# The scaled rows of each image computed on VectorE instead of GpSimd, and two table steps moved ahead of the attention rows

## The chip, the cores and the metric

The kernel runs on one core of a Trainium2 chip. The metric is the device time of one launch in microseconds (us), lower is better. Engine names are those of the profile: PE is TensorE (PEld its weight loads), DVE is VectorE, ACT is ScalarE, POOL is GpSimd, SP is the sync engine, which starts most DMAs.

## The reference, cut to what matters

32 images of 224 x 224 pixels are cut into 1024 patches each, embedded in 64 numbers, passed through one attention head, a layer normalisation, and a feed-forward layer in which each token goes to one of 8 experts. An expert takes the tokens in order, over all images, until its capacity is full.

```python
h = patches @ W.T + b + pos                       # 32 x 1024 x 64
q, k, v = h @ Wq.T + bq, h @ Wk.T + bk, h @ Wv.T + bv
prob = softmax(q @ k.T / 8)                       # per image, 1024 x 1024
h = layernorm(h + prob @ v @ Wo.T + bo)
logits = h @ gate_w + gate_b
idx = argmax(softmax(logits))                     # one of 8 experts
pos = running count of idx over all 32768 tokens
y = relu(h @ w1[idx] + b1[idx]) @ w2[idx] + b2[idx]
out = layernorm(h + nan_to_num(y * prb * (pos < C)))
```

## The kernel before

**Windows.** The program runs in windows b = -2 to 33, one per image. Each engine has its own hand-ordered program `step(b, ...)`, and the engines meet only through semaphores. Window b computes the score matrix of image b, the row maxima of image b+1, the projections of images b+1 and b+2, and the end of attention of image b-1: PE turns the weighted sums to token rows (`turn_sums`, L618), DVE divides them by the softmax sums (`attend`, L1053 to L1058), the residual is added (`residual`, L1387, POOL), ACT squares, DVE sums (`sum_squares`, L1080), ACT takes the root (`norm_root`, L822 and L824), DVE computes the gate (`gate_logits`, `gate_gaps`, `gate_choice`, L1089 to L1111). In window b+1 DVE computes the slots of these tokens (`slot_read`, `probability`, `slot_index`, L1191 to L1206) and POOL scatters the rows to DRAM by indirect DMA (`scatter`, L1411). I count a window from the first matmul of `turn_sums` to that of the next.

**Experts.** From window 6 on, one chunk of four units of 256 tokens of some expert is read back and computed beside each window (`HOST`). Its last steps, all on DVE, are spread over the next two windows: `weigh` (L1213), `finite`, `to_numbers`, `residual_sum`, `centre`, `sum_of_squares`, `scaled` (L1259). POOL writes the finished rows out (`spread_out`, L1424).

**The table.** Every second image (2, 4, ... 28, 30, and 31) DVE works out which units are full and names them for the DMAs. In an even window b from 4 on, `full_units` (L1138 to L1144) and `past_experts` (L1149, L1152) run for image b-2 behind the row maximum of j = 2, and `name_units` follows at j = 3. In the next, odd, window `take_units` (L1182 to L1184) runs behind `attend`. So even windows carry `full_units`, odd ones `take_units`.

**DVE's order in a window.** j counts the eight row maxima (`row_max`, L1031) of the next image; each waits for two matmuls (L563, L565), and the other steps stand between them in a fixed order. Before the first stand `qk_low` (L1023), `shift` (L1037), the slots of image b-2 and, at j = 0, `key_steps` (L1016). ACT waits for `key_steps` to copy the keys (L781), then copies the weighted sums (`u_copy`, L809), and PE's `turn_sums` waits for that copy. The gate stands at j = 6 and 7 (from j = 5 on in windows without a chunk).

**POOL's order in a window** (7 < b < 31): four scatters of image b-2, the residual of image b-1, four scatters, five output transfers, `norm_rows` of image b-1 (rows times reciprocal deviation, 128 x 512, L1398, and the token numbers, 128 x 8, L1399), three output transfers. For images 30 and 31 (`LATE` is 30) the residual and the rows are already on DVE: `last_residual` (L1067) and `last_rows` (L1073, L1074).

Of the kernel before, what the change touches and what calls it, by code (L numbers as in the profile page):

```python
# [12 lines left out]
ALU = mybir.AluOpType  # L13
# [74 lines left out]
def build(nc, x, posT, wqk, wide, deep, w, out):  # L88
    slots = nc.dram_tensor("slots", (SLOTS, ROW), F32, kind="Internal").ap()
    with ExitStack() as ctx:  # L90
# [244 lines left out]
        pool_step = sem("pool_step")  # L335
        sd_ready = sem("sd_ready")
        last_rows_ready = sem("last_rows_ready")
# [45 lines left out]
        PS = 1  # L383
# [379 lines left out]
        def _(act):  # L763
# [52 lines left out]
            def norm_root(n):  # L816
                act.wait_ge(vs_ready, n + 1)
                if n >= 1:
                    act.wait_ge(tail_g, GS * (n - 1) + 1)
                    act.wait_ge(pool_step, min(n, LATE))  # L820
                    after(act, last_rows_ready, n - LATE)
# [138 lines left out]
        def _(dve):  # L960
# [100 lines left out]
            def last_residual(n):  # L1061

                dve.wait_ge(t_ready, n + 1)
                dve.wait_ge(pool_step, PS * LATE)
                after(dve, last_rows_ready, n - LATE)
# [4 lines left out]
            def last_rows(n):  # L1070
                p = n % 2
                dve.wait_ge(scattered[p], of_parity(n - 2, p, 16 * NT))
                dve.tensor_tensor(rows[:, p, :, 0:D], uc[:, :, 0:D], per_token(rstd[:, :], D), ALU.mult)  # L1073
                dve.tensor_scalar(rows[:, p, :, D + 1], rows[:, p, :, D + 1], float(2 * S), None, ALU.add)\  # L1074
                    .then_inc(last_rows_ready, 1)
# [186 lines left out]
            def late_step(n, q, back, done):  # L1262
# [13 lines left out]
                last_rows(n)  # L1276
# [15 lines left out]
            def step(b, c, third, has):  # L1292
# [16 lines left out]
                for j in range(NT):  # L1309
                    if j == 0 and has(2):  # L1310
                        key_steps(b + 2)
                    if has(1):
                        row_max(b + 1, q, j)
                    if j == 1 and has(-1):
                        attend(b - 1, q)
                    if b - 3 in TABLES[:-1] and j == 1:
                        take_units(b - 3)
                    if b - 2 in TABLES[:-1]:
                        if j == 2:
                            full_units(b - 2)  # L1320
# [11 lines left out]
                    if has(-1):  # L1332
# [4 lines left out]
                        if j == 6:  # L1337
                            gate_gaps(b - 1)
                        if j == 7:
# [29 lines left out]
        def _(pool):  # L1369
# [12 lines left out]
            def residual(n, p):  # L1382
# [3 lines left out]
                wait_apart(pool, sq_ready, n)  # L1386
                pool.tensor_tensor(uc[:, :, :], tt[:, :, :], hh[:, p, :, 0:CG], ALU.add)\  # L1387
                    .then_inc(uc_ready, 1)

            def counted(n, i, ins):  # L1390
                ins.then_inc(pool_step, 1)
                wait_apart(pool, pool_step, PS * n + i)

            def norm_rows(n, p):
                pool.wait_ge(rstd_ready, n + 1)
                if n >= 2:
                    pool.wait_ge(scattered[p], of_parity(n - 2, p, 16 * NT))
                pool.tensor_tensor(rows[:, p, :, 0:D], uc[:, :, 0:D], per_token(rstd[:, :], D), ALU.mult)  # L1398
                counted(n, 1, pool.tensor_scalar(rows[:, p, :, D + 1], rows[:, p, :, D + 1], float(2 * S), None,  # L1399
                                                 ALU.add))  # L1400

            def scatter(n, p, tiles):
                if 0 in tiles:
                    wait_apart(pool, prob_ready, n + 1)
                    wait_apart(pool, tail_g, GS * n + GS)
                    if n >= LATE:
# [124 lines left out]
```

## Time and profile before

| | us |
|---|---|
| median of 3 runs (lowest, highest) | 1059.79 (1058.4, 1060.67) |
| the profiled execution | 1059.04 |
| its span in the trace | 1057.1 |
| busy PE, DVE, ACT, POOL | 947.4, 871.8, 712.3, 635.8 |

The span is the time between the first and the last instruction of the profiled execution; 1.9 us of that execution's time lie outside it, and it was 0.75 us faster than the median. TensorE's granted clock is full in all windows that are looked at below (the column PEclk reads 1.00). A row of the timeline gives start, duration, engine, source line and operation, the tile written and those read; in brackets behind it, where there is one, the idle time of the engine before it and what ended it. Start times can overlap the end of the instruction before by some 0.1 us, since an instruction begins while the last results of the one before are still written.

### The profile page before, as it was taken

How to read it: one execution, taken by the hardware profiler on the slowest of the kernel's cores; microseconds unless marked ns; L12 is line 12 of the kernel's file. 1: busy time of each engine (PE TensorE's matmuls, PEld its weight loads, DVE VectorE, ACT ScalarE, POOL GpSimd, SP SyncE). 2: the span in 40 equal slices, each digit the busy share in tenths (PEclk: the TensorE clock that was granted, in tenths of full speed). 3: DMA queues.
4: the chain of work that ended last, by engine and by line, in shares of the span. 5: the costliest groups of instructions: out<-in, count | busy, mean ns of one | idle time of the engine just before them, and what ended most of it. 6: DMA issues, size and time to landing. Idle time of an engine off the chain costs nothing.

```text
span 1057.1 us, 19754 instructions
## 1 busy us (share of the span) xinstructions
PE 947.4 (90%) x6046; PEld 530.7 (50%) x6046; DVE 871.8 (82%) x1711; ACT 712.3 (67%) x1254; POOL 635.8 (60%) x624
## 2 busy tenths in 40 slices
PE   3799999999999999999999999999999999856740
PEld 2355545555555555555555555555555555433420
DVE  3667788789999999999999999999999999675561
ACT  2366655777777777777777777777777776636650
POOL 0004443346666666667776766666666777776775
PEclk9699999999999999999999999999999999958875
DMA  3332224333334333343334333433334332236200
GB/s 95 80 73 58 59 59 107 91 100 101 98 86 120 89 107 99 89 106 103 103 99 107 102 99 86 120 88 107 98 91 106 102 99 72 71 92 177 71 20 10
DMA packets 72504, 96.25 MB, mean 91 GB/s; under 512 B 15923, under 2 KB 52230, under 8 KB 72398
## 3 DMA queue, kind: packets, MB, share of 16 engines
q1 hardware_dynamic: 55566, 77.87, 29.0%
q0 software_dynamic: 16832, 17.11, 5.0%
q8 instruction: 49, 0.80, 0.3%
q14 instruction: 57, 0.47, 0.1%
HBM read 43.68 MB, written 18.11 MB: 58 GB/s over the span
## 4 chain that ended last, share of the span: by engine, by line
PE 48%; DVE 34%; issue 9%; ACT 7%; DMA 1%; POOL 1%; SPq 0%; POOLq 0%; ACTq 0%; DVEq 0%
PE p_u L603 12%; DVE mx L1031 9%; PE p_st L581 8%; PE p_misc L618 6%; PE p_misc L549 4%; PE p_misc L666 3%; PE p_sm L563 3%; PE p_misc L526 3%; ACT uu L809 3%; PE p_st L585 3%; DVE qk L1016 2%; DVE lo L1023 2%; ACT b_h L855 2%; PE p_sm L682 2%; PE p_misc L682 2%
## 5 line engine op out<-in xcount | busy, mean ns | idle before, releaser
L1411 POOL DMA_INDIRECT slots<-rows,idx x256 | 251.9, 984 | 186.2 <-issue 139.6
L1424 POOL DMA_INDIRECT out<-b_o,b_ix x270 | 303.8, 1125 | 98.0 <-issue 74.1
L1031 DVE TENSOR_REDUCE mx<-p_sm 128x1 f32<-128x1024 f32 x252 | 307.1, 1219 | 33.2 <-PE p_sm L565 30.1
L804 ACT ACTIVATE pT<-p_st 128x1024 f32<-128x1024 f32 x256 | 261.9, 1023 | 94.0 <-PE p_st L587 80.1
L603 PE MATMUL p_u<-pT,vv 128*64 128x512 f32 x1024 | 253.5, 605 | 0.0
L581 PE MATMUL p_st<-hi,hx 64*128 64x512 f32 x256 | 126.6, 495 | 8.6 <-ACT pT L804 4.4
L583 PE MATMUL p_st<-hx,hi 64*128 64x512 f32 x256 | 127.1, 496 | 0.0
L603 PEld LDWEIGHTS p_u<-pT,vv 128*64 128x64 f32 x1024 | 61.6, 136 | 104.7 <-issue 92.7
L581 PEld LDWEIGHTS p_st<-hi,hx 64*128 64x128 f32 x256 | 46.9, 183 | 131.3 <-issue 104.0
L563 PE MATMUL p_sm<-kh,hi 64*128 64x512 f32 x252 | 102.4, 406 | 6.1 <-DMA hx<-hi 3.5
L855 ACT ACTIVATE b_h<-p_misc,b_w 128x256 f32<-128x256 f32 x244 | 95.8, 475 | 13.5 <-PE p_misc L666 7.1
L565 PE MATMUL p_sm<-kh,hx 64*128 64x512 f32 x252 | 102.4, 406 | 0.0
L581 PE MATMUL p_st<-lo,hx 64*128 64x512 f32 x256 | 100.5, 392 | 0.0
L583 PE MATMUL p_st<-lx,hi 64*128 64x512 f32 x256 | 100.5, 392 | 0.0
L587 PE MATMUL p_st<-hx,lo 64*128 64x512 f32 x256 | 100.2, 392 | 0.0
L585 PE MATMUL p_st<-hi,lx 64*128 64x512 f32 x256 | 100.2, 391 | 0.0
L1387 POOL TENSOR_TENSOR uc<-tt,hh 128x576 f32<-128x576 f32 x30 | 39.5, 1316 | 77.4 <-DVE tt L1058 77.3
L775 ACT ACTIVATE qk<-p_misc 128x1024 f32<-128x1024 f32 x32 | 32.9, 1027 | 68.8 <-PE p_misc L526 67.5
L549 PE MATMUL p_misc<-w_px,xt 114*128 114x137 f32 x504 | 76.6, 296 | 0.0
L549 PEld LDWEIGHTS p_misc<-w_px,xt 114*128 114x128 f32 x504 | 63.7, 192 | 23.1 <-issue 23.1
L618 PE MATMUL p_misc<-w_j,uu 128*128 128x73 f32 x512 | 64.2, 279 | 9.7 <-ACT uu L809 8.0
L666 PE MATMUL p_misc<-b_xT,b_w 64*128 64x256 f32 x488 | 68.8, 401 | 3.6 <-ACT b_xT L844 1.9
(191 smaller groups left out, 1869.7 us busy)
## 6 DMA issues: line engine op xcount, KB each, us to landing
b_w<-in_w SPq DMA_DIRECT2D x136, 193.5 KB
hx<-hi SPq DMA_DIRECT2D x64, 256.0 KB, 3.4
b_in<-slots SPq DMA_DIRECT2D x136, 66.0 KB
lx<-lo SPq DMA_DIRECT2D x32, 256.0 KB, 3.2
xt<-in_x SPq DMA_DIRECT2D x32, 196.0 KB
out<-b_o,b_ix POOLq DMA_INDIRECT x270, 2.3
kh<-kh SPq DMA_DIRECT2D x32, 128.0 KB, 2.3
lx<-lo SPq DMA_DIRECT2D x32, 128.0 KB, 3.2
```

What stands on the lines that cost most here:

```text
L549: last = pe.matmul(projected(n, r)[:, j // 2, (j % 2) * GP:(j % 2 + 1) * GP], xt[0:KTOK, n % 3, t * P:(t + 1) * P], w_px[:, :], start=True ...
L563: pe.matmul(max_place(n, j)[:, 0, :], hi[t][0:D, j * P:(j + 1) * P], kh[n % 2][0:D, 0:HALF], start=True, stop=True)
L581: pe.matmul(p_st[:, 0, :], hx[t][0:D, kt], upper[t][0:D, 0:HALF], start=first, stop=False, skip_group_check=k > 0)
L583: pe.matmul(p_st[:, 1, :], hi[t][D:P, kt], lower[t][D:P, HALF:S], start=first, stop=False, skip_group_check=k > 0)
L585: pe.matmul(p_st[:, 0, :], lx[t][0:D, kt], hi[t][0:D, 0:HALF], start=False, stop=k > 0, skip_group_check=k > 0)
L603: last = pe.matmul(p_u[c:c + D, a, :], vv[:, p, NT - 1 - k, :], pT[k % 4][:, a * HALF:(a + 1) * HALF], start=(r == 0), stop=(r == 3))
L618: last = pe.matmul(p_misc[:, j // 4, (j % 4) * GT:(j % 4 + 1) * GT], uu[:, j * P:(j + 1) * P], w_j[:, :], start=True, stop=True)
L804: act.activation(pT[k % 4][:, :], flat(p_st), ACT.Exp).then_inc(exp_done, 1)
L855: act.activation(b_h[:, f, u, v, :], place[:, u, v * UNIT:(v + 1) * UNIT], ACT.Relu, bias=b_w[:, r, v, u, W1C + HB * D + f:W1C + HB * D + ...
L1031: dve.tensor_reduce(mx[:, p, at:at + 1], flat(max_place(n, j)), AX.X, ALU.max).then_inc(max_done, 1)
L1411: pool.indirect_dma_start(slots, bass.IndirectOffsetOnAxis(ap=idx[:, p, j:j + 1], axis=0), rows[:, p, j, :], None, bounds_check=SLOTS - 1, ...
L1424: pool.indirect_dma_start(out_rows, bass.IndirectOffsetOnAxis(ap=b_ix[:, o, j:j + 1], axis=0), b_o[:, o, j, :], None, bounds_check=T - 1, ...
```

## The change

`norm_rows` moves from POOL to DVE for all images: in windows up to 30 it runs at j = 6 behind `gate_gaps` and ahead of the row maximum of j = 7. POOL keeps of its arithmetic only the residual sum, so that in windows with chunks its eight output transfers follow each other. One semaphore, `rows_ready`, takes the place of two. Apart from this, `take_units` and `full_units` move from behind `attend` (and, for `full_units`, behind the row maximum of j = 2) to the place ahead of `attend`, behind the row maximum of j = 1.

```diff
@@ scalar, norm_root
                 if n >= 1:
                     act.wait_ge(tail_g, GS * (n - 1) + 1)
-                    act.wait_ge(pool_step, min(n, LATE))
-                    after(act, last_rows_ready, n - LATE)
+                    act.wait_ge(rows_ready, n)
@@ vector
             def last_residual(n):
 
                 dve.wait_ge(t_ready, n + 1)
-                dve.wait_ge(pool_step, PS * LATE)
-                after(dve, last_rows_ready, n - LATE)
+                dve.wait_ge(rows_ready, n)
...
-            def last_rows(n):
+            def norm_rows(n):
                 p = n % 2
-                dve.wait_ge(scattered[p], of_parity(n - 2, p, 16 * NT))
+                dve.wait_ge(rstd_ready, n + 1)
+                if n < 2:
+                    dve.wait_ge(pool_set, 4)
+                else:
+                    dve.wait_ge(scattered[p], of_parity(n - 2, p, 16 * NT))
                 dve.tensor_tensor(rows[:, p, :, 0:D], uc[:, :, 0:D], per_token(rstd[:, :], D), ALU.mult)
                 dve.tensor_scalar(rows[:, p, :, D + 1], rows[:, p, :, D + 1], float(2 * S), None, ALU.add)\
-                    .then_inc(last_rows_ready, 1)
+                    .then_inc(rows_ready, 1)
@@ vector, step
                     if has(1):
                         row_max(b + 1, q, j)
+                    if b - 3 in TABLES[:-1] and j == 1:
+                        take_units(b - 3)
+                    if b - 2 in TABLES[:-1] and j == 1:
+                        full_units(b - 2)
                     if j == 1 and has(-1):
                         attend(b - 1, q)
-                    if b - 3 in TABLES[:-1] and j == 1:
-                        take_units(b - 3)
                     if b - 2 in TABLES[:-1]:
                         if j == 2:
-                            full_units(b - 2)
                             past_experts(b - 2)
...
                         if j == 6:
                             gate_gaps(b - 1)
+                            norm_rows(b - 1)
@@ gpsimd
                 wait_apart(pool, sq_ready, n)
+                wait_apart(pool, rows_ready, n)
                 pool.tensor_tensor(uc[:, :, :], tt[:, :, :], hh[:, p, :, 0:CG], ALU.add)\
                     .then_inc(uc_ready, 1)
...
-            def norm_rows(n, p):
-                pool.wait_ge(rstd_ready, n + 1)
-                if n >= 2:
-                    pool.wait_ge(scattered[p], of_parity(n - 2, p, 16 * NT))
-                pool.tensor_tensor(rows[:, p, :, 0:D], uc[:, :, 0:D], per_token(rstd[:, :], D), ALU.mult)
-                counted(n, 1, pool.tensor_scalar(rows[:, p, :, D + 1], rows[:, p, :, D + 1], float(2 * S), None,
-                                                 ALU.add))
...
-                    if n >= LATE:
-                        pool.wait_ge(last_rows_ready, n - LATE + 1)
-                    else:
-                        wait_apart(pool, pool_step, PS * n + 1)
+                    pool.wait_ge(rows_ready, n + 1)
@@ gpsimd, step
                     scatter(b - 2, par, range(4, NT))
-                    spread_out(done, range(5))
-                    norm_rows(b - 1, 1 - par)
-                    spread_out(done, range(5, NT))
+                    spread_out(done)
...
-                if has(-1):
-                    norm_rows(b - 1, 1 - par)
```

The line numbers of the changed kernel differ by up to 15 (its `row_max` is L1028, `attend` L1050 to L1055, its residual L1390).

DVE at the gate, j = 6 and 7 of an even window with a chunk, before (pri and pm are steps of `gate_gaps`, mx the row maximum, oh and ohs `gate_choice`):

```order
L1101 SCALAR_TENSOR_TENSOR pri<-ld,c_wide 128x64
L1104 TENSOR_REDUCE pm<-pri 128x8
L1031 TENSOR_REDUCE mx<-p_sm 128x1
L1108 TENSOR_TENSOR oh<-pri,pm 128x64
L1111 TENSOR_REDUCE ohs<-oh 128x8
```

and with the change:

```order
L1101 SCALAR_TENSOR_TENSOR pri<-ld,c_wide 128x64
L1104 TENSOR_REDUCE pm<-pri 128x8
L1073 TENSOR_TENSOR rows<-uc,rstd 128x8x64
L1074 TENSOR_SCALAR rows<-rows 128x8
L1028 TENSOR_REDUCE mx<-p_sm 128x1
L1108 TENSOR_TENSOR oh<-pri,pm 128x64
L1111 TENSOR_REDUCE ohs<-oh 128x8
```

Two instructions more stand between the gate's gaps and the last row maximum.

DVE from j = 1 to the table's steps of an even window, before:

```order
L1031 TENSOR_REDUCE mx<-p_sm 128x1
L1053 RECIPROCAL rs<-p_misc 128x8
L1054 SCALAR_TENSOR_TENSOR mk<-hh,rs 128x8
L1056 SCALAR_TENSOR_TENSOR rm<-hh,mk 128x8
L1058 TENSOR_TENSOR tt<-p_misc,rm 128x576
L1031 TENSOR_REDUCE mx<-p_sm 128x1
L1138 TENSOR_SCALAR t_f<-t_cnt 128x8
L1139 TENSOR_TENSOR t_av<-t_f,c_wide 128x8
L1142 TENSOR_TENSOR t_cum<-t_av,c_wide 128x64
L1144 TENSOR_REDUCE t_c<-t_cum 128x8
```

and with the change:

```order
L1028 TENSOR_REDUCE mx<-p_sm 128x1
L1138 TENSOR_SCALAR t_f<-t_cnt 128x8
L1139 TENSOR_TENSOR t_av<-t_f,c_wide 128x8
L1142 TENSOR_TENSOR t_cum<-t_av,c_wide 128x64
L1144 TENSOR_REDUCE t_c<-t_cum 128x8
L1050 RECIPROCAL rs<-p_misc 128x8
L1051 SCALAR_TENSOR_TENSOR mk<-hh,rs 128x8
L1053 SCALAR_TENSOR_TENSOR rm<-hh,mk 128x8
L1055 TENSOR_TENSOR tt<-p_misc,rm 128x576
L1028 TENSOR_REDUCE mx<-p_sm 128x1
```

The four instructions of `full_units` now stand ahead of rs, which is the first that reads the turned sums. In odd windows the three of `take_units` move in the same way from behind tt to ahead of rs.

POOL in a window with chunks, before:

```order
L1387 TENSOR_TENSOR uc<-tt,hh 128x576
L1411 DMA slots<-rows,idx 264448x66 x4
L1424 DMA out<-b_o,b_ix 32768x64 x5
L1398 TENSOR_TENSOR rows<-uc,rstd 128x8x64
L1399 TENSOR_SCALAR rows<-rows 128x8
L1424 DMA out<-b_o,b_ix 32768x64 x3
L1411 DMA slots<-rows,idx 264448x66 x4
```

and with the change:

```order
L1390 TENSOR_TENSOR uc<-tt,hh 128x576
L1399 DMA slots<-rows,idx 264448x66 x4
L1412 DMA out<-b_o,b_ix 32768x64 x8
L1399 DMA slots<-rows,idx 264448x66 x4
L1390 TENSOR_TENSOR uc<-tt,hh 128x576
```

The two arithmetic instructions on `rows` are gone, and nothing stands between the eight output transfers.

## Rows read from the trace of the kernel before

**Rows 1.** The page's chain that ended last, shares of the span by engine.

```profile
PE 48%; DVE 34%; issue 9%; ACT 7%; DMA 1%; POOL 1%; SPq 0%; POOLq 0%; ACTq 0%; DVEq 0%
```

**Rows 2.** Groups by line, DVE: busy us, mean ns | idle before.

```profile
L1089 DVE TENSOR_TENSOR lg<-uc,rstd 128x64 f32<-128x64 f32 x32 | 22.8, 713 | 0.5
...
L1091 DVE TENSOR_TENSOR lb<-lg,c_wide 128x64 f32<-128x64 f32 x32 | 21.1, 659 | 1.1
```

**Rows 3.** Windows: us, busy by engine (instructions), PEclk, DMA share, GB/s.

```profile
116.08:139.98 23.90, 23.67 (x147) 12.41 (x147) 18.81 (x36) 14.42 (x21) 10.19 (x12) 1.00 0.27 66
139.98:164.81 24.83, 23.94 (x146) 12.36 (x146) 21.49 (x44) 14.47 (x21) 10.99 (x12) 1.00 0.25 62
417.35:446.18 28.83, 28.34 (x186) 16.04 (x186) 26.68 (x55) 21.84 (x39) 20.12 (x19) 1.00 0.37 100
446.18:474.56 28.38, 28.03 (x188) 15.95 (x188) 26.33 (x50) 21.73 (x39) 19.03 (x20) 1.00 0.39 102
```

**Rows 4.** Timeline of DVE, window b = 14: start us, us, engine line op.

```profile
419.39 0.21 DVE L1053 RECIPROCAL rs<-p_misc 128x8 f32<-128x8 f32 x1 [1.09 <-PE p_misc L618]
...
421.85 0.38 DVE L1138 TENSOR_SCALAR t_f<-t_cnt 128x8 uint32<-128x8 uint32 x1
...
423.47 0.69 DVE L1213 TENSOR_TENSOR b_p<-p_misc,b_in 128x512 f32<-128x512 f32 x1
...
434.23 1.53 DVE L1089 TENSOR_TENSOR lg<-uc,rstd 128x64 f32<-128x64 f32 x1
...
442.93 1.09 DVE L1016 TENSOR_TENSOR qk<-qk,p_misc 64x896 f32<-64x896 f32 x1
```

**Rows 5.** Timeline of DVE, window b = 15.

```profile
449.74 1.30 DVE L1183 TENSOR_TENSOR t_x<-t_m 128x8 f32<-128x8 f32 x1
...
461.67 1.23 DVE L1031 TENSOR_REDUCE mx<-p_sm 128x1 f32<-128x1024 f32 x1
...
463.18 1.02 DVE L1091 TENSOR_TENSOR lb<-lg,c_wide 128x64 f32<-128x64 f32 x1
...
471.31 1.09 DVE L1016 TENSOR_TENSOR qk<-qk,p_misc 64x896 f32<-64x896 f32 x1
```

**Rows 6.** Timeline of ACT, windows b = 14 and b = 15.

```profile
433.85 0.21 ACT L824 ACTIVATE rstd<-sd 128x8 f32<-128x8 f32 x1
...
473.48 1.03 ACT L809 ACTIVATE uu<-p_u 128x1024 f32<-128x1024 f32 x1
```

**Rows 7.** Timeline of PE, windows b = 14 and b = 15.

```profile
422.77 0.60 PE L643 MATMUL p_misc<-c_wide,b_yT 128*128 128x128 f32 x4
...
461.23 0.39 PE L563 MATMUL p_sm<-kh,hi 64*128 64x512 f32 x1
...
471.13 1.94 PE L603 MATMUL p_u<-pT,vv 128*64 128x512 f32 x8
```

**Rows 8.** Timeline of POOL, windows b = 14 and b = 15.

```profile
433.62 0.97 POOL L1424 DMA_INDIRECT out<-b_o,b_ix  x1 [0.30 <-issue]
434.61 1.06 POOL L1398 TENSOR_TENSOR rows<-uc,rstd 128x512 f32<-128x512 f32 x1
...
449.71 1.31 POOL L1387 TENSOR_TENSOR uc<-tt,hh 128x576 f32<-128x576 f32 x1 [0.86 <-DVE tt L1058]
```

**Rows 9.** Timeline of DVE, window b = 31.

```profile
908.00 0.23 DVE L1089 TENSOR_TENSOR lg<-uc,rstd 128x64 f32<-128x64 f32 x1
...
909.98 0.68 DVE L1073 TENSOR_TENSOR rows<-uc,rstd 128x512 f32<-128x512 f32 x1
...
910.66 0.42 DVE L1220 TENSOR_SCALAR b_fin<-b_p 128x512 uint8<-128x512 f32 x1
```

**Rows 10.** Timeline of POOL, window b = 31.

```profile
907.24 0.97 POOL L1411 DMA_INDIRECT slots<-rows,idx  x1 [0.30 <-issue]
```

**Rows 11.** Timeline of PE and of DVE, window b = 3.

```profile
130.66 0.49 PE L563 MATMUL p_sm<-kh,hi 64*128 64x512 f32 x1
...
131.28 1.22 DVE L1031 TENSOR_REDUCE mx<-p_sm 128x1 f32<-128x1024 f32 x1
```

More of the change, by code:

```diff
@@ L334, in build @@
         set_link = sem("set_link")
-        pool_step = sem("pool_step")
         sd_ready = sem("sd_ready")
-        last_rows_ready = sem("last_rows_ready")
+        rows_ready = sem("rows_ready")
         POOL_SET = 2
@@ L380, in wait_apart @@
                 eng.wait_ge(s, value)
-        PS = 1
         block = ctx.enter_context(nc.Block())
@@ L1275, in late_step @@
                 gate_choice(n)
-                last_rows(n)
+                norm_rows(n)
                 finite(back)
@@ L1386, in residual @@
                 wait_apart(pool, sq_ready, n)
+                wait_apart(pool, rows_ready, n)
                 pool.tensor_tensor(uc[:, :, :], tt[:, :, :], hh[:, p, :, 0:CG], ALU.add)\
                     .then_inc(uc_ready, 1)
-            def counted(n, i, ins):
-                ins.then_inc(pool_step, 1)
-                wait_apart(pool, pool_step, PS * n + i)
-            def norm_rows(n, p):
-                pool.wait_ge(rstd_ready, n + 1)
-                if n >= 2:
-                    pool.wait_ge(scattered[p], of_parity(n - 2, p, 16 * NT))
-                pool.tensor_tensor(rows[:, p, :, 0:D], uc[:, :, 0:D], per_token(rstd[:, :], D), ALU.mult)
-                counted(n, 1, pool.tensor_scalar(rows[:, p, :, D + 1], rows[:, p, :, D + 1], float(2 * S), None,
-                                                 ALU.add))
             def scatter(n, p, tiles):
```

## The prediction

> **What bounds the kernel now.** The first view is the chain of waits that ended last: 48% of it is PE and 34% DVE [rows 1], so neither alone sets the time. The table of windows, read next, shows two kinds in steady state: even windows, which carry `full_units`, take 28.83 us, odd ones, with `take_units`, 28.38 us [rows 3]. What ends each is seen in the timeline. In window 14 DVE sits idle once, 1.09 us before rs, for PE's turned sums [rows 4]; that wait belongs to a loop that DVE itself starts: `key_steps` (qk), the copy of the keys on ACT, the copy of the weighted sums, `turn_sums`. From qk at 442.93 [rows 4] to the window's end at 446.18 it is 3.25 us, and from qk at 471.31 [rows 5] to the end at 474.56 [rows 3] again 3.25. So a window ends 3.25 us after qk, and what counts is when DVE reaches qk.
>
> Three things let DVE start late again within a window, whatever it saves ahead of them. b_p needs PE's transposes of L643, which begin at 422.77 and take 0.60, while b_p starts at 423.47 [rows 7, 4]: 0.10 us behind them. The row maximum of j = 6 needs PE's L563, in window 15 from 461.23 on for 0.39, and starts at 461.67 [rows 7, 5]. And lg needs ACT's rstd, which ends at 434.06 in window 14, while lg starts at 434.23 [rows 6, 4]. So **savings ahead of lg hardly count, and those from lg to qk count fully**, until PE is the limit: in window 15 PE's weighted sums end at 473.07 [rows 7], ACT's copy of them starts at 473.48 [rows 6], which leaves some 0.4 us.
>
> From lg to qk there is one odd thing. lg and lb are 128 x 64 operations that take 0.23 and 0.22 us in window 31 or where nothing disturbs them [rows 9], but lg takes 1.53 in window 14 [rows 4] and lb 1.02 in window 15 [rows 5]. Beside them POOL multiplies the rows: from 434.61 for 1.06 us, to 435.67 [rows 8], and lg ends at 435.76. The means of all 32, 713 and 659 ns [rows 2], say how often: twelve lg of 1.53 (windows 8 to 30, even) and twenty of 0.23 make 22.9 us, where the group has 22.8. For lb eleven of 1.02 (9 to 29, odd), seven of 0.95 (1 to 7) and fourteen of 0.22 make 21.0 against 21.1. DVE is held while POOL's multiplication runs.
>
> **The change, part by part.** *The rows on DVE.* Windows 31 and 32 do it already: from the start of rows at 909.98 to the next instruction at 910.66 it is 0.68 us for both instructions [rows 9]. I take 0.68. The bounds are 0.60 (the multiplication is partly covered) and 0.88 (it is itself held for 0.2, as much as t_f is in window 14 [rows 4], below).
>
> *The multiplication off POOL.* With it goes the hold: 1.53 - 0.23 = 1.30 us in twelve windows, 1.02 - 0.22 = 0.80 in eleven, 0.95 - 0.22 = 0.73 in seven. Window 31 speaks for this directly: lg at 908.00 takes 0.23 while a row transfer of POOL runs from 907.24 to 908.21 [rows 9, 10], so the transfers that will follow each other now do not hold it. The Trainium skill ("SBUF — State Buffer", section "SBUF: two separate sides") calls the ports that DVE and GpSimd share an exclusive lock, kept for a whole instruction by whoever starts first; the trace agrees that lg is blocked and not merely slowed, but not on the order, since lg began 0.38 us ahead of the multiplication in window 14. By that rule the 0.38 would be someone else's, and the even windows would give back 0.92 instead of 1.30, which makes the sum below -4.7 instead of -9.3.
>
> *Even windows 8 to 30.* Between lg and qk: -1.30 + 0.68 = -0.62. `full_units` moves from behind tt into the 1.09 us idle: from t_f at 421.85 to b_p at 423.47 it is 1.62 us [rows 4]; in them lie a hold of 0.2 by the residual (t_f takes 0.38 where an operation of 8 columns takes some 0.17) and the two operations of `past_experts`, some 0.43, so its own four need 1.0 undisturbed and fit into the 1.09. But b_p then waits for PE and gains only some 0.03. Together -0.65, twelve times: **-7.8 us**. If the order in front of b_p let the whole 1.0 through, this would be the rival of PE below.
>
> *Odd windows 9 to 29.* -0.80 + 0.68 = -0.12, eleven times: **-1.3 us**. `take_units`, held now by the residual (t_x 1.30 at 449.74 [rows 5], POOL's residual from 449.71 for 1.31 [rows 8]), goes into the idle time too, but the row maximum of j = 6 waits for PE at 461.23 + 0.39 in any case. Nothing from it. Window 7, -0.73 + 0.68: -0.05.
>
> *Windows without a chunk, 1 to 5.* There the gate's logits stand ahead of the row maximum of j = 6 and the rows behind it. The 0.73 saved is hidden, because that maximum then waits for PE; the 0.68 lies open. The last maximum starts at 131.28, PE's matmuls for it end at 131.15 [rows 11], and with the rows it starts at about 131.53: **+0.24** in each of windows 1, 2, 3 and 5, about +1.0. Window 4 carries `full_units` and takes 24.83 us, where window 3 takes 23.90 [rows 3], with the table's count (0.2) that window 4 doesn't have: the table's steps behind tt cost it 1.1. The move frees them, less the 0.24: -0.85. Window 6 has the same steps, but a chunk on PE beside them, and PE leads again sooner; I grant a third, -0.3.
>
> *POOL.* It loses 1.06 and 0.25 us of work per window and the wait around them, and its last three output transfers start earlier. It sits idle before the next scatter, and nobody waits for the output buffers, four of which go round. Nothing. *New waits.* On DVE `norm_rows` waits for rstd, which lg has waited for already, and for the scatter of image b-3, which POOL did in the first half of the window before. Behind it stand the last row maximum, the gate's choice, the shift and qk; it would cost all of them, but it is long over. The residual now waits for `rows_ready` of the image before, given a window earlier. *The end,* from window 31 on, has the same instructions and moves as one piece.
>
> Sum: -7.8 - 1.3 - 0.05 + 1.0 - 0.85 - 0.3 = **-9.3 us**. The profiled execution took 1059.04, its span 1057.1; it becomes 1049.7. The median of the runs stands 0.75 above it, so I predict 1050.5.
>
> **Rivals.** *PE becomes the limit everywhere.* If more of the table's move counts than I grant, or DVE loses other small holds, windows shrink to where the copy of the weighted sums follows PE at once: 0.4 us less in odd windows, and 28.83 - 27.95 = 0.9 in even ones. 12 x 0.9 + 11 x 0.4 = 15.2, with the early part near 0: about 1044.5. For it: the idle time of PE in window 15 is small, so the floor is well known. Against: b_p, the sixth maximum and lg each start within 0.2 us of what they wait for. 10%.
>
> *Part of the hold stays.* lg is held from 434.23, when POOL's row transfer (433.62 to 434.59 [rows 8]) was still running. If such transfers, now back to back, hold two-input operations of DVE, those 0.38 us stay in the twelve even windows: 12 x 0.38 = 4.6 of the 9.3 are lost, 1055. If the odd windows lose 0.2 as well, 2.2 more go, and it can't be told from no change. Against: lb in windows 9 to 29 and lg in window 31. 14%.
>
> *Slower: the hold isn't the multiplication's.* If it comes from POOL's turn from transfers to anything else, or from whatever POOL issues beside the gate, lg and lb stay as long as they are, and DVE has 0.68 us more between lg and qk: 23 windows x 0.68 and five early ones x 0.7, less 0.9 for window 4, make +18: 1078. It decides once more than 0.62 of the 1.30 us stays. For it: the 0.38 us by which lg began first. Against: lg in window 31 [rows 9], and that lb ends right behind the multiplication in each odd window. 7%. (That the change does nothing at all is excluded: the instructions do move.)
>
> **How the numbers follow.** My forecast has 69%, with a range of its own of 1047 to 1054 from the bounds of the rows (28 x 0.2 = 5.6 up, of which I take two thirds, since both ends would have to hold in every window, and 28 x 0.08 = 2.2 down) and 1 us for the early part. The range that should hold 8 in 10 reaches to the two rivals on the faster side and leaves out the slow one: 1045 to 1056. A measurement of this kernel can tell about 0.2%, 2.1 us, from no change. Faster by more than that: 69 + 10 + 10 of the 14 = 89%; within it 4%; slower 7%.
>
> **What would show it.** lg and lb at 0.23 in all windows; rows on DVE at 0.68; even windows at 28.2 and odd ones at 28.26; windows 1, 2, 3 and 5 longer by 0.2 and window 4 at 24.0; DVE idle before b_p and before the sixth maximum, and hardly any before rs. Wrong would be: lg still above 0.6; even windows at 27.9; a wait of DVE for scattered rows; idle time on DVE before rs as now, with a later tt because the table's steps overran it.

## The result, and the profile after

| | us |
|---|---|
| changed kernel, median of 4 runs (lowest, highest) | 1050.14 (1049.75, 1052.52) |
| kernel before, 4 runs beside it | 1059.1 (1057.93, 1060.67) |
| ratio, 95% interval | 0.9922 (0.9911 to 0.9934) |
| profiled execution after, its span | 1052.52, 1050.7 |
| busy PE, DVE, ACT, POOL after | 945.6, 854.0, 708.1, 586.2 |

The change saves 9 us, 0.8%. The first view is the table of windows after, with columns as in [rows 3]: windows 3 and 4, then 14 and 15.

```profile
117.72:141.92 24.20, 23.84 (x148) 12.40 (x148) 18.87 (x38) 14.43 (x21) 9.14 (x9) 1.00 0.25 64
141.92:165.96 24.04, 23.82 (x146) 12.36 (x146) 21.32 (x46) 14.43 (x21) 9.13 (x9) 1.00 0.25 64
...
415.44:443.65 28.21, 28.04 (x186) 15.97 (x186) 26.07 (x57) 21.61 (x39) 18.13 (x17) 1.00 0.38 103
443.65:471.94 28.29, 28.03 (x188) 15.93 (x188) 25.44 (x52) 21.61 (x39) 17.29 (x17) 1.00 0.39 102
```

Against [rows 3], window 14 is 0.62 shorter and window 15 0.09, window 4 is 0.79 shorter and window 3 0.30 longer. Why is seen in the groups by line of DVE after (they answer to [rows 2]).

```profile
L1073 DVE TENSOR_TENSOR rows<-uc,rstd 128x512 f32<-128x512 f32 x32 | 22.1, 692 | 1.0
L1213 DVE TENSOR_TENSOR b_p<-p_misc,b_in 128x512 f32<-128x512 f32 x26 | 18.0, 691 | 27.5 <-PE p_misc L641 27.5
L1149 DVE TENSOR_TENSOR t_ge<-c_wide,t_c 128x64 f32<-128x64 f32 (+2 forms) x16 | 9.3, 579 | 0.1
L1091 DVE TENSOR_TENSOR lb<-lg,c_wide 128x64 f32<-128x64 f32 x32 | 7.2, 225 | 1.1
L1089 DVE TENSOR_TENSOR lg<-uc,rstd 128x64 f32<-128x64 f32 x32 | 7.1, 221 | 0.5
L1050 DVE RECIPROCAL rs<-p_misc 128x8 f32<-128x8 f32 x32 | 6.6, 207 | 19.3 <-PE p_misc L616 19.3
```

lg and lb have fallen to 7.1 and 7.2 us from 22.8 and 21.1 [rows 2], 29.6 less together, and 22.1 us of rows have come onto DVE. DVE's whole busy time even falls, from 871.8 to 854.0: the rows took the place of time in which DVE stood blocked. The next fence is the timeline of DVE in window 14 after; [rows 4] has the same window before.

```profile
417.54 0.21 DVE L1050 RECIPROCAL rs<-p_misc 128x8 f32<-128x8 f32 x1 [0.28 <-PE p_misc L616]
...
419.99 0.43 DVE L1149 TENSOR_TENSOR t_ge<-c_wide,t_c 128x64 f32<-128x64 f32 x1
...
421.56 0.69 DVE L1213 TENSOR_TENSOR b_p<-p_misc,b_in 128x512 f32<-128x512 f32 x1 [0.86 <-PE p_misc L641]
...
432.34 0.22 DVE L1089 TENSOR_TENSOR lg<-uc,rstd 128x64 f32<-128x64 f32 x1
...
433.87 0.69 DVE L1073 TENSOR_TENSOR rows<-uc,rstd 128x512 f32<-128x512 f32 x1
...
440.40 1.09 DVE L1013 TENSOR_TENSOR qk<-qk,p_misc 64x896 f32<-64x896 f32 x1
```

And this is window 15 after, beside [rows 5].

```profile
449.71 0.69 DVE L1213 TENSOR_TENSOR b_p<-p_misc,b_in 128x512 f32<-128x512 f32 x1 [1.43 <-PE p_misc L641]
...
459.15 1.22 DVE L1028 TENSOR_REDUCE mx<-p_sm 128x1 f32<-128x1024 f32 x1
...
468.69 1.09 DVE L1013 TENSOR_TENSOR qk<-qk,p_misc 64x896 f32<-64x896 f32 x1
```

A window can be read as **three legs**: from its first matmul to b_p (PE's projections and transposes lead), from b_p to qk (DVE works with pauses of 0.1 us at most), from qk to the next window's first matmul (the loop over ACT and PE). Taken from the start times of these three instructions, in us:

| | window 14 | window 15 |
|---|---|---|
| before | 6.12 + 19.46 + 3.25 = 28.83 | 6.24 + 18.89 + 3.25 = 28.38 |
| after | 6.12 + 18.84 + 3.25 = 28.21 | 6.06 + 18.98 + 3.25 = 28.29 |

The last leg stands still in both. In the even window the first leg does too, and the gain is all in the middle one. In the odd window the first leg is 0.18 shorter and the middle one 0.09 longer.

The page's chain that ended last, after (before: [rows 1]):

```profile
PE 51%; DVE 29%; issue 9%; ACT 8%; DMA 1%; POOL 1%; SPq 0%; POOLq 0%; ACTq 0%; DVEq 0%
```

### The profile page after: what moved, and what is told of

Its sections match the earlier page's. It is cut to its first block, busy times and chain, and to the rows that moved or that the text cites. A ratio compares the mean times of both kernels' runs of the same rounds, so it can differ in the third digit from the quotient of the medians.

```text
span 1050.7 us, 19710 instructions
## 1 busy us (share of the span) xinstructions
PE 945.6 (90%) x6046; PEld 530.5 (50%) x6046; DVE 854.0 (81%) x1771; ACT 708.1 (67%) x1254; POOL 586.2 (56%) x564
## 4 chain that ended last, share of the span: by engine, by line
PE 51%; DVE 29%; issue 9%; ACT 8%; DMA 1%; POOL 1%; SPq 0%; POOLq 0%; ACTq 0%; DVEq 0%
PE p_u L601 14%; PE p_st L579 9%; DVE mx L1028 8%; PE p_misc L616 6%; PE p_misc L547 4%; PE p_misc L664 3%; ACT uu L807 3%; PE p_sm L561 3%; PE p_st L583 3%; DVE lo L1020 2%; DVE qk L1013 2%; PE p_misc L524 2%; PE p_sm L680 2%; ACT b_h L852 2%; PE p_misc L680 1%
## 5 line engine op out<-in xcount | busy, mean ns | idle before, releaser
L1412 POOL DMA_INDIRECT out<-b_o,b_ix x270 | 294.7, 1091 | 86.7 <-issue 81.7
L1028 DVE TENSOR_REDUCE mx<-p_sm 128x1 f32<-128x1024 f32 x252 | 306.9, 1218 | 35.1 <-PE p_sm L563 33.7
L1390 POOL TENSOR_TENSOR uc<-tt,hh 128x576 f32<-128x576 f32 x30 | 39.3, 1312 | 80.3 <-DVE tt L1055 80.3
```

The costliest lines, as they stand in the source:

```text
L1028: dve.tensor_reduce(mx[:, p, at:at + 1], flat(max_place(n, j)), AX.X, ALU.max).then_inc(max_done, 1)
L1412: pool.indirect_dma_start(out_rows, bass.IndirectOffsetOnAxis(ap=b_ix[:, o, j:j + 1], axis=0), b_o[:, o, j, :], None, bounds_check=T - 1, ...
```

## The experiments

Experiments 1 to 4 ran on one chip, beside the kernel before at 1059.65 us (median of 17 runs).

**1. The rows alone.** The changed kernel with the table's steps put back behind `attend`.

```diff
...
-                    if b - 3 in TABLES[:-1] and j == 1:
-                        take_units(b - 3)
-                    if b - 2 in TABLES[:-1] and j == 1:
-                        full_units(b - 2)
                     if j == 1 and has(-1):
                         attend(b - 1, q)
+                    if b - 3 in TABLES[:-1] and j == 1:
+                        take_units(b - 3)
...
```

(and `full_units` again at j = 2.)

> The rows on VectorE as in the change, the table's steps left behind the attention rows. My theory: lg and lb fall to 0.23 us in every window as in the change; odd windows stay at 28.3 us, because the held t_x (1.3 us) is hidden behind the wait of the sixth row maximum; even windows are some 0.05 us longer than the change's 28.21; window 4 is longer by 1.1 and window 6 by 0.3 to 0.7. In all 1.4 to 2.2 us slower than the changed kernel, so about 1052, 7 to 8 us under the kernel before. Rival (the table's move carries the gain): the time stays within 3 us of the kernel before, and even windows stay above 28.6.

Measured 1052.6 us (6 runs, 1050.36 to 1055.53), ratio 0.9935 (0.9918 to 0.9951). Its windows 14 and 15:

```profile
418.57:446.80 28.23, 28.01 (x185) 15.93 (x186) 26.07 (x57) 21.57 (x39) 18.16 (x17) 1.00 0.38 103
446.80:475.13 28.33, 28.03 (x188) 15.97 (x188) 26.38 (x52) 21.59 (x39) 17.26 (x17) 1.00 0.39 101
```

The groups by line say what the table's steps do in their old place:

```profile
L1183 DVE TENSOR_TENSOR t_x<-t_m 128x8 f32<-128x8 f32 x15 | 15.0, 999 | 0.5
L1138 DVE TENSOR_SCALAR t_f<-t_cnt 128x8 uint32<-128x8 uint32 x15 | 8.2, 550 | 0.0
...
L1050 DVE RECIPROCAL rs<-p_misc 128x8 f32<-128x8 f32 x32 | 6.6, 208 | 37.2 <-PE p_misc L616 37.2
```

t_x, an operation of eight columns, takes 1.0 us on average beside POOL's residual sum, and still windows 14 and 15 are those of the changed kernel but for 0.02 and 0.04 us; what the table's old place costs is seen in window 4, which takes 24.91 us here and 24.04 after the change, and in window 7, 28.84 against 28.28, where the last of the three steps of `take_units` is the one held, for 1.91 us. Windows 1 to 31 sum to 7.0 us less than before; the changed kernel's to 9.41 less. The rows are three quarters of the gain. The time is within the forecast of about 1052.

**2. The table's steps alone.** The kernel before with these two steps in front of `attend`, the rows still on POOL (the edit above turned round, on the kernel before).

> The table's steps ahead of the attention rows as in the change, the rows left on GpSimd. My theory: window 4 falls from 24.83 to 23.8, window 6 by 0.3 to 0.7, even windows from 28.83 to 28.78, odd ones stay at 28.38: 1.5 to 2.5 us under the kernel before, about 1057. lg in even windows stays at 1.5. Rival (the table's move carries the gain, by 0.6 per even window): about 1051 with even windows at 28.2.

Measured 1059.05 us (11 runs, 1056.45 to 1061.31), ratio 0.9991 (0.9979 to 1.0002): no difference that can be told. DVE's groups keep the hold:

```profile
L1089 DVE TENSOR_TENSOR lg<-uc,rstd 128x64 f32<-128x64 f32 x32 | 22.1, 690 | 0.5
L1091 DVE TENSOR_TENSOR lb<-lg,c_wide 128x64 f32<-128x64 f32 x32 | 21.4, 670 | 1.1
```

Window 14 is 28.84 us as before, window 4 is 23.71 (1.12 shorter), window 6 is 0.45 and window 8 0.28 shorter, and the odd windows from 9 on are some 0.04 longer each; the sum of the windows falls by 1.4. So the move pays where it was forecast to, in the first windows with a table, and not in the later ones. The time is 0.6 us under the kernel before, less than the 1.5 to 2.5 forecast. With the 7.0 of experiment 1 the two halves make 8.4 of the 9.41 us. More than half of what is missing is in window 7, which loses 0.52 in experiment 1, as said there, and nothing in the changed kernel.

**3. The hold put back.** The changed kernel, and on POOL, in the old place of the rows (behind the fifth output transfer), a multiplication of a constant tile of 448 columns that nothing reads. DVE's program is that of the changed kernel.

```diff
+            def beside(n):
+                pool.wait_ge(rstd_ready, n + 1)
+                pool.tensor_tensor(s_io[:, :, :], s_io[:, :, :], s_io[:, :, :], ALU.mult)
...
-                    spread_out(done)
+                    spread_out(done, range(5))
+                    beside(b - 1)
+                    spread_out(done, range(5, NT))
...
+                if has(-1):
+                    beside(b - 1)
...
```

> The changed kernel, and in the old place on GpSimd one multiplication of 448 columns of a constant tile that nobody reads, behind the same wait for rstd. If the hold is that of GpSimd's multiplication: lg is held again in the even windows (1.2 to 1.5 us) and lb in the odd ones (0.9 to 1.0), now on top of the rows on VectorE; even windows 29.3 to 29.5, odd ones 28.9 to 29.1; in all 20 to 26 us slower than the changed kernel, 1070 to 1076. If the hold came with the rows' data or from the transfers: no change against 1050, lg and lb at 0.23.

Measured 1078.02 us (4 runs, 1076.69 to 1078.81), ratio 1.0174 (1.0158 to 1.019). The timeline of POOL and of DVE in window 14:

```profile
440.20 0.95 POOL L1397 TENSOR_TENSOR s_io<-s_io 128x448 f32<-128x448 f32 x1
```

```profile
439.83 1.42 DVE L1090 TENSOR_TENSOR lg<-uc,rstd 128x64 f32<-128x64 f32 x1
441.28 0.29 DVE L1092 TENSOR_TENSOR lb<-lg,c_wide 128x64 f32<-128x64 f32 x1
```

The middle leg of window 14 becomes 20.14 us (18.84 after the change), that of window 15 19.76 (18.98). The windows are as forecast (29.49 and 29.07); the whole is 2 us above the forecast of 1070 to 1076, and windows 29 and 30, at a granted clock of 0.94 where the other kernels have 1.00, lose 2.4 and 2.8 us each to the changed kernel. The two kernels share DVE's program and every transfer. What differs is the multiplication, POOL's wait for rstd and the break in its transfers; experiment 4, on the same chip, keeps the last two and takes 28.0 us less. So about 28 us are the price of one multiplication a window on another engine that no one waits for. It is also what the rival "slower" would have cost (1078).

**4. Written, not read.** The same place on POOL holds two memsets of 256 and 192 columns instead.

```diff
-                pool.tensor_tensor(s_io[:, :, :], s_io[:, :, :], s_io[:, :, :], ALU.mult)
+                pool.memset(s_io[:, 0:4, :], 0.0)
+                pool.memset(s_io[:, 4:NT - 1, :], 0.0)
```

> As the run before, but GpSimd fills the tile (two memsets of 256 and 192 columns) instead of multiplying it: it occupies GpSimd in the same place without reading SBUF. If it takes a GpSimd operation that reads SBUF to hold VectorE's two-input operations (the Trainium skill, page SBUF - State Buffer, section SBUF: two separate sides, has it so): lg and lb at 0.23, time 1050 as the changed kernel. If any GpSimd operation on a tile holds them: lg or lb longer by the length of the memsets (0.3 to 0.8 us), 1055 to 1066.

Measured 1050.02 us (4 runs, 1049.46 to 1051.75), ratio 0.9909 (0.9895 to 0.9924). POOL in window 15, then DVE:

```profile
459.12 0.34 POOL L1397 MEMSET s_io<- 128x256 f32 x1
459.37 0.29 POOL L1398 MEMSET s_io<- 128x192 f32 x1
```

```profile
459.23 0.23 DVE L1092 TENSOR_TENSOR lb<-lg,c_wide 128x64 f32<-128x64 f32 x1
```

lb runs inside the first memset and takes the 0.23 us it has alone. POOL's wait for rstd and the break in its transfers are here as in experiment 3; the reading of SBUF and the arithmetic are gone (and a third of the duration), and with them the hold. The run doesn't tell the reading from the arithmetic. It agrees with the Trainium skill ("SBUF — State Buffer", section "SBUF: two separate sides"), which has a two-input operation of VectorE shut out only by a GpSimd operation that reads SBUF. The odd windows are 28.3 to 28.4 us, up to 0.1 above the changed kernel's. In window 15 this 0.1 arises behind `norm_rows`, over a us after the memsets (oh takes 0.28 where it had 0.21); its cause stays open.

**5. to 8. A chip with a low granted clock.** To see whether more could be had, I wrote three further variants: the rows one window later, behind `key_steps` (5); the same with one scatter less ahead of POOL's residual (6); and 5 with the residual sum on DVE as well, so that POOL does no arithmetic (7). The changed kernel went along (8). The first edit:

```diff
...
+                    if j == 0 and has(-2):
+                        norm_rows(b - 2)
...
                             gate_gaps(b - 1)
-                            norm_rows(b - 1)
...
```

> The changed kernel once more, as the measure for the three runs beside it: 1050.1 within 0.2%.

> The rows of image b-1 are computed on VectorE not at j = 6 of window b but in window b+1, behind the row maximum of j = 0, ahead of the wait for the turned sums. The instructions are the same. My theory: 0.68 us between lg and qk counts fully until TensorE is the limit, and between qk and lg it is hidden, so windows 7 to 29 all fall to 27.9 to 28.05 (28.21 and 28.28 before the move), windows 1 to 5 by 0.1 to 0.3: 5 to 7 us less than the changed kernel, about 1044. Rival (work on VectorE counts wherever it stands): 1050, windows as in the changed kernel. Rival (the later scatters, by 2 us, hold up GpSimd's residual and with it ScalarE's squares): windows longer than 28.3.

> As the run before, with three scatters ahead of GpSimd's residual instead of four, so that the residual doesn't come later. If the residual's start matters: faster than the run before by 1 us or more. My theory: the same within 1 us, since ScalarE squares the sum at j = 3, over a us behind it in either case.

> As e5_rows_next_window, and the residual sum of all images on VectorE too, behind the attention rows (0.73 us more there, less the holds of t_ge and t_da, 0.3 us in even windows). My theory: it stands where VectorE idles for TensorE (0.86 us ahead of b_p in even windows, 1.43 in odd ones), so nothing changes against e5_rows_next_window, within 1.5 us. If VectorE's sum of work counts: 24 windows x 0.4 to 0.7, 10 to 17 us slower.

In that job the kernel before took 1327.24 us (11 runs, 1313.66 to 1331.02) at a mean granted clock of about 0.88, where it had 0.95 elsewhere. The changed kernel took 1390.44 (ratio 1.049, 1.0442 to 1.0537), variant 5 1422.6 (1.0709, 1.0655 to 1.0763), 6 1432.82 (1.0791, 1.0746 to 1.0837) and 7 1455.06 (1.0984, 1.0939 to 1.103). Nothing of the forecasts can be judged by these; what they show of the chip stands in the last section. Variants 5 and 7 were therefore run again on another chip, where before took 1060.08 us (11 runs).

**9. The rows one window later, again.**

> The kernel of e5_rows_next_window once more, because in that job the chip gave TensorE a mean clock of 0.84 to 0.89 and the kernel before took 1327 us. On a chip on which the kernel before takes 1060 us, my theory gives windows 7 to 29 of 27.9 to 28.05, windows 1 to 5 shorter by 0.1 to 0.3 than the changed kernel's, 1044 in all. The rival, that VectorE's work counts wherever it stands: 1050, windows of 28.21 and 28.28. If the chip holds TensorE back again: the order of the job before, this kernel 7% above the kernel before.

Measured 1076.13 us (5 runs, 1072.94 to 1076.3), ratio 1.0152 (1.0134 to 1.0169): the theory of 1044 fell. What came true is the rival that the expectation of variant 5 names last, that the later scatters hold up the residual. The timeline of POOL, one row from window 2 and two from window 14, and that of ACT in window 2:

```profile
99.76 1.34 POOL L1393 TENSOR_TENSOR uc<-tt,hh 128x576 f32<-128x576 f32 x1
...
433.41 0.97 POOL L1402 DMA_INDIRECT slots<-rows,idx  x1 [5.10 <-DVE rows L1074]
...
438.26 1.33 POOL L1393 TENSOR_TENSOR uc<-tt,hh 128x576 f32<-128x576 f32 x1
```

```profile
101.14 0.63 ACT L812 ACTIVATE sq<-uc 128x512 f32<-128x512 f32 x1 [2.93 <-POOL uc L1393]
```

The first scatter needs the rows, and the residual stands behind four scatters (six in windows 2 to 7). Later rows make the residual late, by 2.1 us in window 14 and 3.2 in windows 2 to 6. In window 14 it then falls on t_da, which is held for 1.80 us from 437.82, ahead of b_p; in window 2 ACT waits 2.93 us for it and DVE 3.16 for ACT, and that window takes 27.68 us, against 23.84 in the changed kernel. PE stands still meanwhile, and the granted clock, 1.00 in all of window 2 in the changed kernel, falls (rows of the table of windows):

```profile
101.00:102.00 1.00, 0.00 (x0) 0.00 (x0) 0.20 (x1) 0.86 (x3) 0.83 (x2) 1.00 0.00 0
...
104.00:106.00 2.00, 2.00 (x10) 0.85 (x8) 0.57 (x1) 1.00 (x2) 0.00 (x0) 0.50 0.05 17
```

So a part of what windows 2, 3, 5 and 6 lose comes by the clock, which is 0.94 or 0.95 over each of them. Windows 1 to 7 have 17.6 of the 24.1 us that windows 1 to 31 lose to the changed kernel. From 8 on the even ones lose 0.6 to 1.0 each, and the odd ones win 0.2: there the rows' later place pays. The cost of the move was queued on an engine that the move itself does not touch.

**10. No arithmetic on POOL, again.** As 9, with the residual of every image on DVE.

```diff
...
                     if j == 1 and has(-1):
                         attend(b - 1, q)
+                        last_residual(b - 1)
...
-                    scatter(b - 2, par, range(4))
-                    residual(b - 1, 1 - par)
-                    scatter(b - 2, par, range(4, NT))
+                    scatter(b - 2, par, range(NT))
...
```

(The windows without a chunk change in the same way.)

> The kernel of e7_no_arithmetic_on_gpsimd once more, for the same reason. My theory: as e8_rows_next_window_again within 1.5 us, since the sum stands where VectorE waits for TensorE. The rival: 10 to 17 us slower than that run. If the chip holds TensorE back again: 10% above the kernel before.

Measured 1043.81 us (5 runs, 1042.19 to 1045.99), ratio 0.9845 (0.9826 to 0.9863), the fastest kernel of this study. It is 32 us faster than 9, so both readings of the expectation fell, which took 9 to be free of the residual's delay. Windows 14 and 15, DVE's qk of window 14, and the chain of the page:

```profile
412.88:440.92 28.04, 27.98 (x185) 15.88 (x185) 26.53 (x58) 21.57 (x39) 15.93 (x16) 1.00 0.40 103
440.92:469.01 28.09, 28.03 (x188) 15.96 (x188) 26.04 (x53) 21.59 (x39) 17.16 (x16) 1.00 0.41 103
```

```profile
437.68 1.09 DVE L1013 TENSOR_TENSOR qk<-qk,p_misc 64x896 f32<-64x896 f32 x1 [0.49 <-ACT qk L773]
```

```profile
PE 77%; ACT 9%; DVE 5%; issue 5%; DMA 1%; POOL 1%; SPq 0%; POOLq 0%; ACTq 0%; DVEq 0%
```

DVE now waits at qk for the queries that PE and ACT make. The legs of window 14 are 6.14 + 18.66 + 3.24: without its wait of 0.49 the middle one is 18.17, that is, 18.84 less the 0.68 of the rows. So the rows' time came out in full, and PE and ACT let 0.18 of it through. The end of the middle leg has passed from DVE to PE, whose share of the chain is 77%. This is the floor that the rival "PE becomes the limit everywhere" spoke of (27.95; 28.06 measured).

**11. and 12. The residual alone on VectorE.** The changed kernel, rows at j = 6, with only the residual moved as in 10. The first run met another chip on which the granted clock was low, so the kernel was run twice.

> The changed kernel with the residual sum of all images moved from GpSimd to VectorE as well, straight behind the attention rows of its window; the scaled rows stay where the change put them, and GpSimd is left with its transfers alone. Theory, the changed kernel's windows are set by VectorE's chain between the residual operand and the last norm: the sum (0.69 us on VectorE, from the rows' multiplication of the same shape) stands where VectorE idles for TensorE's first projection (0.86 us in window 14 and 1.43 in window 15 of the changed kernel), so it is free, and only the holds of 0.2 to 0.4 us ahead of it go: windows 28.1 to 28.3, 1048 to 1051 us. Rival 1, VectorE's sum of work sets the pace, so that each added operation costs itself less the hold: +0.4 us a window from 6 on, 1060. Rival 2, what made the kernel without GpSimd arithmetic 6 us faster was GpSimd's freedom alone and not the rows' later place: windows 28.06 and 1044 here too.

Beside a kernel before of 1316.75 us it took 1409.56 (ratio 1.0701, 1.0657 to 1.0746), which judges none of the three readings.

> The same kernel as e10, since its runs met a TensorE that was held back (before took 1316.75 us beside it). If before takes about 1059 us again, the three readings are as there. Theory, the sum stands in time that VectorE idles for TensorE's first projection: windows 28.1 to 28.3, 1048 to 1051 us. Rival 1, VectorE's sum of work sets the pace: +0.4 us a window, 1060. Rival 2, GpSimd's freedom alone made the kernel of e9 fast: windows 28.06, 1044. If before takes over 1300 us again, this one takes about 1410, and that says only that the order of the kernels turns in that condition.

Measured 1051.31 us (5 runs, 1049.7 to 1052.99) beside 1059.97, ratio 0.9916 (0.99 to 0.9931): the first theory. DVE in window 14:

```profile
417.65 0.76 DVE L1063 TENSOR_TENSOR uc<-tt,hh 128x576 f32<-128x576 f32 x1
...
419.46 0.21 DVE L1149 TENSOR_TENSOR t_ge<-c_wide,t_c 128x64 f32<-128x64 f32 x1
...
420.23 0.69 DVE L1213 TENSOR_TENSOR b_p<-p_misc,b_in 128x512 f32<-128x512 f32 x1 [0.35 <-PE p_misc L641]
...
439.10 1.09 DVE L1013 TENSOR_TENSOR qk<-qk,p_misc 64x896 f32<-64x896 f32 x1
```

The sum takes 0.76 us (the 0.69 of the expectation was read at 512 columns, and the sum has 576), and in window 14 it costs 0.03: the wait before b_p shrinks from 0.86 to 0.35 us and t_ge loses its hold of 0.2. The legs are 6.12 + 18.87 + 3.25. DVE's busy time rises from 854.0 to 870.5 us. Windows 1 to 31 sum to 1.25 us more than the changed kernel's. All of that is in five even windows (8, 10, 18, 22 and 26) of 28.49 us, where the others have 28.24. In these five b_pos takes 0.66 or 0.67 us, and 0.42 in window 14; the last section has more on b_pos. With 9 and 10 this makes a square of four kernels (before took 1059.1 to 1060.08 beside each):

| us | residual on POOL | residual on DVE |
|---|---|---|
| rows at j = 6 | 1050.14 | 1051.31 |
| rows in the next window | 1076.13 | 1043.81 |

Moving the rows out of the middle leg is worth 7.5 us, but only once the residual no longer stands behind the scatters; moving the residual is worth nothing by itself. The four ran in three jobs on different chips, so differences of 1 us between them mean little.

## Why the prediction was right

The forecast was 1050.5 us with a range of 1045 to 1056; the median is 1050.14. The sums by kind of window, each against before from the start times of `turn_sums`:

| windows | forecast | measured |
|---|---|---|
| even, 8 to 30 | -7.8 | -7.56 |
| odd, 9 to 29 | -1.3 | -1.31 |
| 7 | -0.05 | -0.04 |
| 1, 2, 3, 5 | +1.0 | +0.66 |
| 4 | -0.85 | -0.79 |
| 6 | -0.3 | -0.39 |
| sum (with +0.02 in 31) | -9.3 | -9.41 |

- **The hold is the multiplication's, and goes with it.** Shown from both sides: lg and lb are at 0.22 in the changed kernel and rise to 694 and 618 ns on average when experiment 3 puts a multiplication back; experiment 4 shows that it isn't POOL's turn from transfers to something else.
- **Rows cost 0.68.** 0.69 in the timeline. From lg to qk, window 14 takes 8.06 us, against 8.70 from [rows 4]: -0.64, forecast -0.62. In window 15, from the maximum of j = 6 (the prediction's "sixth") to qk, it is 9.54 against 9.64 in [rows 5]: -0.10, forecast -0.12.
- **Savings ahead of lg hardly count.** lg stands 16.88 us behind the start of window 14 before and 16.90 after, the maximum of j = 6 in window 15 15.49 and 15.50. DVE now idles 0.86 and 1.43 us before b_p, as forecast. In window 15 b_p itself comes 0.18 earlier and the time is lost again before that maximum: 0.13 where DVE's sum of squares waits for ACT, 0.09 at b_pos, which takes 0.66 instead of 0.57. The third wait that the prediction names, lg for rstd, was misread for window 14: DVE's own maximum of j = 6 runs from 433.10 to 434.31 there and lg follows it in order, so rstd at 434.06 held up nothing. From b_p to lg it is 10.76 us before and 10.78 after; b_p alone does the work of all three in the even windows.
- **The wait before rs** was forecast to vanish nearly; it falls from 1.09 to 0.28 us in window 14.
- **Part of the hold stays** was a rival with 14%. On lg nothing stays, the 0.38 us by which it began ahead of the multiplication included: it takes 0.22. But a hold did go elsewhere: the residual sum, which used to meet t_f and t_x, now meets t_ge (0.43) and t_da (0.23). Neither costs anything, since both stand in the time before b_p.
- **Windows 1, 2, 3 and 5** cost 0.12, 0.11, 0.30 and 0.13 instead of 0.24 each. The prediction took the 0.73 saved at lb as hidden. Of it 0.54 was not: in window 3 the maximum of j = 6 starts 12.77 us into the window against 13.30 before, and waits 0.21 for PE. The rows then take 0.68, and the last maximum starts 0.15 later (15.36 us into the window against 15.20 in [rows 11]), where 0.25 was forecast. Windows 1, 2 and 5 show the same within 0.02; in window 3 another 0.13 comes before idx. So the small term was right within a factor of two by a wrong step.
- **The even windows' -7.8** is met in part by luck. Windows 8 and 10 gain 0.89 each, since b_c had started 0.27 later there before than in window 14; window 30 gains only 0.30. The other nine gain 0.54 to 0.64, where 0.65 was forecast.
- **The profiled execution** was forecast at 1049.7 and took 1052.52, although its windows gave the 9.41. Its first window starts 1.41 us later and its tail is 1.60 longer. Before the first window the two programs are the same; between 40 and 50 us the granted clock was 0.67, against 0.81 before, in these rows of the table of windows (after, then before):

```profile
40.00:50.00 10.00, 8.22 (x31) 3.98 (x31) 4.14 (x5) 6.05 (x6) 0.00 (x0) 0.67 0.29 67
```

```profile
40.00:50.00 10.00, 8.21 (x37) 3.55 (x36) 5.12 (x5) 6.07 (x6) 0.00 (x0) 0.81 0.28 65
```

The spans of the other three runs are 1048.0, 1048.1 and 1048.6, so most of the 3 us is this execution's and not the change's. The tail varies by itself: experiment 2, whose tail is that of the kernel before, has one 0.94 us longer. What lengthened it was not tried.

## What to carry to other kernels

Before moving work to a busy engine, ask how much of its busy time is blocked time: an operation that takes 1.53 us in one place and 0.23 in another is waiting for something, and the neighbour's instruction that ends with it names what. Cut the period into legs between the instructions that wait for another engine. Work added where the engine idles before such a wait was nearly free here (0.76 us cost 0.03 in window 14), and work taken out of a leg without a wait counted in full (0.62 of 0.62) until TensorE became the limit (experiment 10). And follow a moved operation through the queue of each engine that consumes it: the same step was worth -7.5 us or +26 us by what stood behind it on GpSimd.

## What the runs showed of the hardware

**A held operation can begin before what holds it.** lg starts at 439.83 in experiment 3, the multiplication on POOL at 440.20, and lg ends at 441.25, 0.10 us after it; t_da of experiment 9 starts 0.44 us before the residual and ends 0.03 after it. In both cases a transfer of POOL ended just before its operation. By the records, then, the one that starts first does not win, as the prediction saw for lg in window 14; whether POOL takes hold of SBUF earlier than its recorded start can't be told from them. The row maxima, which read PSUM, run undisturbed beside the residual: that of window 14 after, from 418.86 on, takes 1.21 us.

**A one-input operation takes longer where a transfer of POOL ends beside it.** In the odd windows 9 to 29 after the change, b_pos takes 0.65 to 0.67 us, in the even ones 0.41 or 0.42. In window 15:

```profile
452.55 0.97 POOL L1399 DMA_INDIRECT slots<-rows,idx  x1 [0.30 <-issue]
```

```profile
453.12 0.66 DVE L1221 TENSOR_SCALAR b_pos<-b_p 128x512 f32<-128x512 f32 x1
```

In each of these windows a transfer of POOL ends while b_pos runs, and b_pos ends 0.25 us later, 0.05 before the next transfer starts; where none ends beside it, it has its 0.42. b_fin, of the same shape, runs beside the middle of that transfer and takes 0.42, and the two-input lg of window 15 has a transfer end beside it (at 460.56) and takes 0.23. No run was made to try it.

**On two chips the order of the kernels turned round.** Where the granted clock was low, the kernel before was the fastest of all: 1327 us before, 1390 changed, 1423 to 1455 the variants; and 1317 against 1410 (the kernel of 11) on the second such chip. The kernel before, the changed one and variant 7 stand in the reverse of the order that they have elsewhere (1060, 1050, 1044). The changed kernel there, window 14, and that of variant 7, window 14 too, in the table of windows:

```profile
501.96:542.93 40.97, 31.12 (x186) 17.69 (x186) 26.53 (x57) 21.67 (x39) 17.31 (x18) 0.88 0.27 71
```

```profile
528.99:573.73 44.74, 32.24 (x186) 17.75 (x186) 27.07 (x58) 21.73 (x39) 15.72 (x16) 0.81 0.25 65
```

DVE and ACT do the same work within 0.6 us of their busy time elsewhere. PE is busy 31 and 32 us, not 28, at the lower clock, and 10 and 12.5 us of the windows pass with PE idle. The timeline of the changed kernel has such a pause. DVE rests from 515.41, ACT from 516.79 and PE from 518.99; DVE and ACT are released by nothing that the profile knows, and PE follows ACT:

```profile
525.26 1.02 ACT L802 ACTIVATE pT<-p_st 128x1024 f32<-128x1024 f32 x1 [8.47 <-remote]
525.30 1.23 DVE L1028 TENSOR_REDUCE mx<-p_sm 128x1 f32<-128x1024 f32 x1 [9.89 <-remote]
...
526.34 0.79 PE L579 MATMUL p_st<-hi,hx 64*128 64x512 f32 x1 [7.35 <-ACT pT L802]
```

The table of windows has the granted clock in the pause:

```profile
520.00:522.00 2.00, 0.00 (x0) 0.00 (x0) 0.00 (x0) 0.00 (x0) 1.60 (x2) 1.00 0.20 57
522.00:524.00 2.00, 0.00 (x0) 0.00 (x0) 0.00 (x0) 0.00 (x0) 0.97 (x1) 0.59 0.47 132
524.00:526.00 2.00, 0.00 (x0) 0.00 (x0) 0.70 (x1) 0.74 (x1) 0.00 (x0) 0.50 0.00 0
```

The clock is still full when all three engines rest, and it falls within the pause; POOL goes on with its transfers up to 523.18. So the low clock follows this pause and does not begin it. Why those chips did this, and whether the pauses are what turns the order, stays open; no run was made for it.
